# Differential attention: the four attends of a group issued as two pairs, at steps 2 and 6 of TensorE's order

## The reference, cut to what matters

```python
def _L1_attn_b_ref(x, Wq, bq, Wk, bk, Wv, bv, Wp, bp, lambda_q1, lambda_k1, lambda_q2, lambda_k2):
    H, H2, hd = (16, 8, 8)                       # 16 heads of 8 features
    q = (x @ Wq.T + bq).reshape(Bb, Nn, H, hd).transpose(0, 2, 1, 3)
    k = (x @ Wk.T + bk).reshape(Bb, Nn, H, hd).transpose(0, 2, 1, 3)
    v = (x @ Wv.T + bv).reshape(Bb, Nn, H, hd).transpose(0, 2, 1, 3)
    ...
    a1 = softmax(q1 @ k1.T * scale); x1 = a1 @ v1      # heads 0 to 7
    a2 = softmax(q2 @ k2.T * scale); x2 = a2 @ v2      # heads 8 to 15
    out = concatenate([x1 - lv * x2, x2], axis=-1) @ Wp.T + bp
...
x = x + _L1_attn_b_ref(_layernorm(x), ...)             # Nn = 512 tokens, Bb = 8 sequences
```

## Time and profile before

| | us |
|---|---|
| median of 3 runs | 2715.28 (2713.32 to 2717.45) |
| profiled execution | 2702.93 |
| its span, first to last instruction | 2701.1 |
| steps of this layer, group 0 to the last | about 1902 to 2375 of the span |

### The profile page before, as it was taken

How to read it: one execution, slowest core, us unless ns; L and a number is a source line. 1 busy time by engine, 2 the same in 40 slices (tenths; PEclk the granted TensorE clock), 3 DMA queues, 4 the chain that set the end, 5 groups by cost and what they waited for, 6 DMA issues and landing times. The chain is left out here.

```text
span 2701.1 us, 40094 instructions
## 1 busy us (share of the span) xinstructions
PE 2417.3 (89%) x12716; PEld 1529.1 (57%) x12716; DVE 1928.1 (71%) x4454; ACT 1413.1 (52%) x2280; POOL 1453.0 (54%) x1357
## 2 busy tenths in 40 slices
PE   4477997998789889979999989998999999979999
PEld 3344564666756566644444467776444444447777
DVE  6865775775677667756666578887787778758887
ACT  4642454333435533346666455554677677655554
POOL 5924654333365634356666545554776576425554
PEclk8788898998979989999999999998999999989999
DMA  1001111221011022210000021110000000022221
GB/s 48 0 3 29 36 37 57 95 89 56 1 47 42 14 93 91 95 57 1 1 1 1 26 84 64 56 56 32 1 1 1 2 1 1 1 79 68 71 67 44
DMA packets 57513, 104.50 MB, mean 39 GB/s; under 512 B 15192, under 2 KB 30424, under 8 KB 57048
## 3 DMA queue, kind: packets, MB, share of 16 engines
q1 hardware_dynamic: 57304, 101.90, 12.0%
HBM read 86.53 MB, written 2.62 MB: 33 GB/s over the span
## 5 line engine op out<-in xcount | busy, mean ns | idle before, releaser
L4469 POOL TENSOR_TENSOR l_moe1sc<-l_moe1s,l_moe1bcs 128x512 f32<-128x512 f32 x192 | 281.5, 1481 | 223.3 <-ACT l_moe1s L4291 204.0
L2327 DVE TENSOR_REDUCE l_diffneg_max<-psum 128x1 fp32r<-128x512 f32 x512 | 335.3, 685 | 92.1 <-PE psum L2065 84.2
L2242 ACT ACTIVATE l_diffweights<-psum 128x1024 f32<-128x1024 f32 x256 | 262.0, 1026 | 131.6 <-PE psum L2094 130.4
L4291 ACT ACTIVATE l_moe1s<-psum 128x512 f32<-128x512 f32 x256 | 152.5, 597 | 212.2 <-PE psum L851 209.3
L4380 DVE TENSOR_TENSOR x<-l_moe1sc,psum 128x512 f32<-128x512 f32 x256 | 174.6, 682 | 97.6 <-POOL l_moe1sc L4469 57.1
L2065 PE MATMUL psum<-l_diffkz,l_diffQ 128*128 128x512 f32 (+1 forms) x512 | 234.9, 477 | 3.8 <-DVE l_diffneg_max L2327 2.7
L2866 ACT ACTIVATE l_lightswapped<-psum 32x512 f32<-32x512 f32 x304 | 179.0, 589 | 100.9 <-DVE l_lightturned L2958 97.4
L4387 DVE TENSOR_TENSOR l_moe1g_lo<-x,l_moe1g_hi 128x512 fp32r<-128x512 f32 x256 | 221.7, 867 | 0.4 <-ACT l_moe1g_hi L4266 0.2
L1592 DVE TENSOR_REDUCE l_attn0neg_max<-psum 128x1 fp32r<-128x512 f32 x256 | 167.3, 683 | 52.8 <-PE psum L1326 50.1
L1498 ACT ACTIVATE l_attn0weights<-psum 128x1024 f32<-128x1024 f32 x128 | 130.3, 1024 | 120.4 <-PE psum L1348 120.4
L4291 ACT ACTIVATE l_moe0s<-psum 128x512 f32<-128x512 f32 x144 | 85.8, 596 | 200.0 <-PE psum L851 178.1
(11 more groups left out here) (584 smaller groups left out, 6706.4 us busy)
## 6 DMA issues: line engine op xcount, KB each, us to landing
l_moe0bcs<-gate_rows SPq DMA_DIRECT2D x64, 512.0 KB, 4.5
l_moe1bcs<-gate_rows SPq DMA_DIRECT2D x64, 512.0 KB, 3.9
l_attn0Q<-l_attn0q_hi SPq DMA_DIRECT2D x128, 64.0 KB, 2.0
l_moe1w_raw<-in_moe_w SPq DMA_DIRECT2D x20, 256.0 KB, 6.9
l_attn0Q<-l_attn0q_lo SPq DMA_DIRECT2D x64, 64.0 KB, 2.0
l_moe0w_raw<-in_moe_w SPq DMA_DIRECT2D x20, 128.0 KB, 5.1
x<-in_x SPq DMA_DIRECT2D x8, 256.0 KB, 5.0
out<-x SPq DMA_DIRECT2D x8, 256.0 KB, 2.3
```

Source lines behind the costliest of these rows:

```text
L2242: nc.scalar.activation(weights[:, tt, 2 * pair:2 * pair + 2, :], ps[:, S[m % 2]:S[m % 2] + 2, :], ACT.Exp, scale=SCALE).then_inc(act_exp.s ...
L2327: nc.vector.tensor_reduce(neg_max[:, n % 2, st, row:row + 1], ps[:, bank_of(("max", n, b)), :], AXX, ALU.max, negate=True).then_inc(vec_ma ...
L4291: nc.scalar.activation(s[:, n % 2, h, :], ps[:, H1[(n * HT + h) % 2], :], ACT.Silu).then_inc(act_silu.sem, act_silu.step("silu", h))
L4469: nc.gpsimd.tensor_tensor(sc[:, n % 2, h, :], s[:, n % 2, h, :], weights_row(n), ALU.mult).then_inc(pool_sc.sem, pool_sc.step("sc", h))
```

## The change

The attend at step 0 moves to step 2, where it stands directly ahead of the one that was there; the attend at step 4 moves to step 6, likewise. Steps 0 and 4 have nothing between their two maxima. The work and the number of instructions stay; the orders of ScalarE, VectorE, GpSimd and the DMA queues are unchanged, and so is the ring's order.

```diff
                     for m in range(8):
                         scores(i, G, m, whole)
                         scores_for_max(i, *block_at(G, m, 0), last, whole)
-                        if m == 0 and behind:
-                            attend(i, G - 1, 2)
                         if m == 1:
                             project(i, G + AHEAD, "q", last)
...
                         if m == 2 and behind:
+                            attend(i, G - 1, 2)
                             attend(i, G - 1, 3)
                         if m == 3:
                             project(i, G + AHEAD, "k", last)
-                        if m == 4:
-                            attend(i, G, 0)
                         if m == 5:
                             max_rows(i, G + 1, last)
                         if m == 6:
+                            attend(i, G, 0)
                             attend(i, G, 1)
```

## The result

Over 9 runs each, the changed kernel takes 2733.6 us (2728.9 to 2741.8) and the one before 2715.3 us: a ratio of 1.0066, with a 95% interval of 1.0043 to 1.0089, so 18 us slower (12 to 24). The direction was forecast, and 2733.6 lies in the range 2723 to 2755; the forecast of +25 us was 7 too high.

The account below looks back on a forecast made before the run. TensorE was taken as the bound. Added waits less saved shape changes gave +3.24 us a sequence, 25.9 for eight, less 1 at the end: +25 on the 2715.3 median makes 2740 us, range 2723 to 2755.

Parts of the forecast that it names:

- TensorE is the bound and nearly without waits: Whole layer: TensorE busy 462.4 of 474 us, with one wait of 0.17 us in a plain group, at step 0.
- the walk: Step-by-step reckoning of a group's starts, each matmul waiting for the bank three places before; +3.24 us a sequence, chance 0.75.
- The saved change of shape, 0.14 a pair: Paired attends at steps 2 and 6 save array shape changes: 0.28 us a group, 9.0 in the layer, bounds 0 and 18.
- The exponentials and the output copy: Moved attends at steps 2 and 6 make no exponential wait, and ScalarE has slack for the output copy; cost nothing.
- The waits, by step: Short steps make TensorE wait for reductions and, at step 4, the copy of k; waits grow 0.99 us a plain group.
- The split of the two pairs: Forecast for each move alone: step 0's attend 60.8 us a sequence, about +16 in all; step 4's 59.7, +8.
- The last group and a half have no maxima left and so no waits: less 1: Layer's end: no maxima remain there, so no waits are added, and 1 us comes off the sum.
- The clock, put at 0.04 and once a sequence: Rival: new waits lower TensorE's clock once a sequence, adding 8 x 3 = 24 us, 2764 in all; chance 0.04.
- The base: Starting time for the sum: the median of 2715.3 us, 12 above the profiled execution's 2702.9.
- The other side (-9): Rival: banks and VectorE's queue absorb the short steps, leaving only the saved shape changes, -9.0 us, 2706; chance 0.07.

Follow-up runs that it names:

- halved kernels: Every maximum reduced over 256 of its 512 columns: in the kernel before 2689.0 us (ratio 0.9892), in the changed kernel 2699.4 us (0.9923).
- the two single moves: Against the kernel before, only one attend moved: step 0 to step 2, 2731.1 us; step 4 to step 6, 2717.6 us.
- both kernels with fillers: One unread 128x512 matmul for each of 24 maxima left out at the layer's end: kernel before 2727.5 us, changed kernel 2742.3 us.

## Why the prediction came out as it did

- **TensorE is the bound and nearly without waits: right.** With less for VectorE to do, the old order gains 1.6 us a sequence of 58.7, and no more (the walk had 57.4 for 57.15). In the plain group it is 0.18 (13.35 for 13.53), the one wait of 0.17 that the prediction had read.
- **The saved change of shape, 0.14 a pair: borne out.** The pairs last 1.92, as in the earlier trace rows, and from their start to that of the maximum behind them it is 1.86 (2190.17 to 2192.03), the 0.86 and 1.00 of the walk. The halved kernels show hardly any further cost of a strip and a whole maximum side by side; of the bounds, 0 and 0.28 a pair, neither was near.
- **The exponentials and the output copy: right** in the middle of the layer, nothing waits for them anew.
- **The waits, by step: right in place, their sum too large.** Steps 0 to 2 wait for reductions, step 4 for the copy of k, step 6 hardly. The plain group came to +0.51 instead of +0.71: 0.08 of that was in the base of the walk (13.45 for 13.53) and most of the rest at steps 5 and 6, where 0.15 of waits was expected and 0.04 measured (scores of step 6 at 10.86, their strip maximum at 10.90). The group with the statistics has +0.73 instead of +1.04, that with the next sequence's transposes +0.48 for +0.67, and that with `end` and `values` +0.79 for +0.82. A sequence thus came to +2.51 us for the walk's +3.24. (The distances that the prediction then lists for the second and third kind of group, 14.9 and 14.7, do not follow from its own terms: 13.75 + 1.04 and 14.23 + 0.67 give 14.8 and 14.9. Measured are 14.48 and 14.71.) Seven sequences make 17.6 us. That this is so near the 18 of the medians is partly luck: between single profiles the layer grew by 28.8 or by 13, and the rest of it cancels only against a base that itself varies.
- **The split of the two pairs: right in order.** 1.63 and 0.90 us a sequence, where the walk gave about 2.1 and 1.0 (60.8 and 59.7 for 58.7).
- **"The last group and a half have no maxima left and so no waits: less 1": this step failed.** The changed kernel needs 8.8 us more there than the undisturbed kernel before, and 2.3 less than the other execution of it. The prediction looked for waits for maxima only. What the runs show is a wait for the exponentials in the last distance (about 1.5 us) and, for the larger part (some 7 us), a lowered clock.
- **The clock, put at 0.04 and once a sequence: rightly set aside for the middle, missed at the end.** In the middle it is at 1.00 (1935 to 2145 and 2165 to 2350), as the earlier trace rows let expect. In the last two distances it comes down in both profiles of the changed kernel and in one of two of the kernel before; it also does so in those of the two single moves, of the halved changed kernel and of both kernels with fillers, and stays up in the halved kernel before, with the old order at the end, and with the pairs behind the whole maximum. The Trainium skill, TensorE: Matmul & The Clock Gate, section on a second failure mode with a cycling PSUM queue, names such swings for short idles between groups of matmuls; in this layer they are seen only in its last three groups. The other fall, at the loop's turn, stands behind over 3 us of idle time in both kernels.
- **The base.** The sum was put on the median of before, 12 us over its profiled execution. In the one other execution that was profiled, 15.8 of its 17 us more lie in this layer, most of them at its end, at a lowered clock. The changed kernel already has a fall there, so part of what an ordinary execution of before loses is not added to it again; how often before has the fall was not counted.
- **The other side (-9)** needed added waits under 0.28 a group; in the plain group they were 0.79 (0.51 net and the 0.28 saved).

## What to carry to other kernels

Where two engines hand work over through few buffers, the spacing of other work between the handovers matters as much as its amount. Here three banks, each 0.6 us of work for VectorE, could not keep VectorE busy through 1.9 us of attends, nor let TensorE through two short steps without a wait. Before merging long pieces to save a switch, walk the release of each buffer through the new order, with start-to-start times from the trace; here it named each place in the middle of the layer, and its sum was 30% too high; it did not see the end, where the work is of another kind and the clock falls. And compare totals only after a second profile of the base: two executions of the same kernel were 17 us apart, nearly as much as the change was worth.

## What the runs showed of the hardware that was not expected

- Reductions of 128x512 from PSUM last 0.685 us, but six in a row take 3.85, 0.63 from start to start (four take 2.47 in the earlier trace rows, 0.59); the duration of a single one is longer than what each adds in a row.
- Nearly the same stretch, with the same 123 matmuls, runs in 21.0 us at a mean granted clock of 1.00 and in 32.1 at 0.54, in one kernel. Ahead of the fall TensorE had 0.23 us of idle time and eight matmuls of 16 columns, as it had in the execution without a fall.
- In the second of these the lowered clock lasts for some 34 us (0.50 from 2351.7 to 2385.7) while TensorE is busy nearly throughout (33.66 of 34.20 us by the records, 2351.70 to 2385.90).
- In the changed kernel one plain group of every second sequence in the loop takes 14.39 instead of 14.04. There the product behind the reciprocal starts 1.61 behind the transposes (2116.57) and not 1.25, so 0.36 late, and the whole maximum of step 0 with it:

```profile
2118.18 0.29 DVE L2339 TENSOR_TENSOR l_diffon<-psum,l_diffrec 128x128 f32<-128x128 f32 x1 [0.48 <-DVE l_diffrec L2335]
...
2118.52 0.19 PEld L2065 LDWEIGHTS psum<-l_diffkz,l_diffQ 128*128 128x128 f32 x1 [0.75 <-DVE l_diffon L2339]
```

The kernel before has the same delay, at 2108.38 and 2232.15, and there the attend of step 0 hides it: these groups take 13.53 and 13.51. Where the delay comes from was not looked into.
